# Two FFN stages of a fused kernel: rotations ahead of scalings at the end of a row, the MLP's norm earlier at its start

## The reference

```python
h = shift_token(x)                      # channels 64..127 from one token earlier
q, k, v = jnp.split(h @ wqkv, 3, axis=-1)   # 8 heads of 64
q = l2norm(q) * qs
k = l2norm(k) * ksc
q, k = rotary_xpos(q, k)
o = local_attention(q, k, v)            # windows of 64, each sees itself and the one before
x = x + o @ wo
h = shift_token(x)
h = (h - mu) / jnp.sqrt(var + 1e-05) * lg + lb
a, g = jnp.split(h @ w1 + b1, 2, axis=-1)
x = x + (a * jax.nn.gelu(g)) @ w2 + b2
```

## Time and profile before

| | |
|---|---|
| runs of the kernel | 2509.22, 2513.75, 2514.84 us (median 2513.75) |
| the profiled execution | 2516.16 us, span 2514.3 us, 43414 instructions |
| mean granted clock of TensorE | 0.885 |
| TensorE busy | 1950.6 us (78%) |
| VectorE busy | 1599.0 us (64%) |
| ScalarE busy | 1240.2 us (49%) |
| GpSimd busy | 1070.4 us (43%) |

### The profile page before, as it was taken

The page is one execution under the profiler, slowest core; times in us unless marked ns, Lnnn a source line. Parts: engine busy times, 40 slices in busy tenths (PEclk is TensorE's granted clock), DMA queues, the critical chain, the costliest instruction groups (busy, mean ns, idle before and its releaser), DMA issues.

```text
span 2514.3 us, 43414 instructions
## 1 busy us (share of the span) xinstructions
PE 1950.6 (78%) x14880; PEld 1224.8 (49%) x14880; DVE 1599.0 (64%) x2479; ACT 1240.2 (49%) x2826; POOL 1070.4 (43%) x838
## 2 busy tenths in 40 slices
PE   2788888858888986588888873896687888884596
PEld 1555555424555553355555532683344644642485
DVE  6677777556899796677777736584443344335486
ACT  2466655438999795465555543343322222224242
POOL 2555555335777675445655515132231033003333
PEclk9799999886999798789999985798898999896798
DMA  6000000020000001000000021204000000000202
GB/s 213 2 1 1 2 2 2 1 83 16 24 20 24 18 25 41 1 1 2 2 1 2 1 71 62 56 22 142 0 0 0 1 0 0 0 0 14 66 22 67
DMA packets 43928, 63.32 MB, mean 25 GB/s; under 512 B 7504, under 2 KB 33488, under 8 KB 42736
## 3 DMA queue, kind: packets, MB, share of 16 engines
q1 hardware_dynamic: 39232, 51.96, 6.6%
q0 software_dynamic: 4544, 9.35, 1.2%
HBM read 45.26 MB, written 21.18 MB: 26 GB/s over the span
## 4 chain that ended last, share of the span: by engine, by line
issue 30%; PE 19%; DVE 5%; ACT 3%; DMA 1%; SPq 1%; POOL 1%; DVEq 0%; POOLq 0%; ACTq 0%
PE PS L1721 3%; PE PS L448 2%; PE PS L1703 2%; PE PS L1705 1%; PE PS L1704 1%; DVE arena L756 1%; PE PS L1711 1%; PE PS L482 1%; DVE arena L769 1%; ACT arena L635 1%; PE PS L500 1%; PE PS L318 1%; PE PS L471 1%; DMA arena<-sorted_x 1%; PE PS L412 1%
## 5 line engine op out<-in xcount | busy, mean ns | idle before, releaser
L1495 POOL TENSOR_TENSOR arena<-arena 128x1024 f32<-128x1024 f32 x128 | 299.6, 2362 | 131.7 <-ACT arena L1429 131.7
L947 POOL TENSOR_TENSOR arena<-arena 128x512 f32<-128x512 f32 x128 | 132.8, 1040 | 263.7 <-DVE arena L790 261.8
L635 ACT ACTIVATE arena<-PS,arena 128x128 f32<-128x128 f32 x512 | 180.3, 370 | 125.3 <-DVE arena L783 124.9
L318 PE MATMUL PS<-arena_r 128*128 128x512 f32 x216 | 125.5, 581 | 135.2 <-DVE arena L756 63.8
L756 DVE SCALAR_TENSOR_TENSOR arena<-PS,fcol,big 128x512 f32<-128x512 f32 x256 | 177.3, 741 | 53.9 <-ACT arena L611 46.1
L1403 PE MATMUL PS<-con,arena 128*128 128x128 f32 x1024 | 157.2, 298 | 48.4 <-DVE arena L1479 46.0
L1479 DVE COPY arena<-PS 128x512 f32<-128x512 f32 x256 | 165.6, 684 | 21.3 <-PE PS L1403 21.2
L1403 PEld LDWEIGHTS PS<-con,arena 128*128 128x128 f32 x1024 | 118.8, 150 | 121.3 <-issue 94.6
L1429 ACT ACTIVATE arena<-PS,arena 128x512 f32<-128x512 f32 x256 | 154.9, 688 | 43.8 <-DVE arena L1460 42.1
L1440 ACT ACTIVATE arena<-arena 128x512 f32<-128x512 f32 x256 | 162.5, 636 | 23.3 <-DVE arena L1467 17.2
L2023 POOL DMA_INDIRECT expert_y<-arena x78 | 74.7, 958 | 209.3 <-DVE arena L1982 205.6
(11 more groups left out here) (366 smaller groups left out, 4924.3 us busy)
## 6 DMA issues: line engine op xcount, KB each, us to landing
big<-in_gu SPq DMA_DIRECT2D x16, 512.0 KB, 8.4
sorted_x<-in_slots SPq DMA_DIRECT2D x2, 2515.5 KB, 15.5
arena<-sorted_x SPq DMA_DIRECT2D x6, 774.0 KB, 7.6
big<-in_dn SPq DMA_DIRECT2D x16, 256.0 KB, 8.7
arena<-expert_y SPq DMA_DIRECT2D x16, 256.0 KB, 3.3
big<-in_wqkv SPq DMA_DIRECT2D x2, 1536.0 KB, 8.2
arena<-q_split SPq DMA_DIRECT2D x96, 32.0 KB
arena<-k_split SPq DMA_DIRECT2D x96, 32.0 KB
```

Of the source, the lines that this page charges most:

```text
L318: pe.matmul(bank, w_hi, hi, start=first, stop=False)
L635: act.activation(pr[:, u % 2, t, :], PS[:, u % 2, t * P:(t + 1) * P], ACT.Exp, bias=nmax[:, u % 2, t:t + 1], accum_out=psum_[:, u % 2, t:t ...
L947: g.tensor_tensor(pn[:, u % 2, :, :], pr[:, u % 2, :, :], pinv[:, u % 2, :].unsqueeze(2).broadcast_to([P, TPB, P]), ALU.mult).then_inc(s(" ...
L1495: g.tensor_tensor(a, a, mk[:, hp, 2 * half:2 * half + 2, :], ALU.mult).then_inc(s("a_masked"), 1)
```

## The change

On TensorE, the row's last values go ahead of the third norm's sum; at the start of the row, the MLP's mean goes ahead of the third value projection, and the variance ahead of the scores. On ScalarE, `hidden_input` moves to the end of the row before, the square ahead of the second unit's exponentials, and the last `take_heads` ahead of the third norm. On VectorE, the MLP's centring goes ahead of the copies of values, and `scaled(r, 3)` behind both; at the end of the row, the third and the fourth rotation go ahead of the first and the second scaling. POOL's list is the same, and nothing is added or removed.

```diff
@@ ffn_pe, row(r) @@
-                project_values(r, 0, 1, 2)
+                project_values(r, 0, 1)
                 if p is not None:
                     hidden_mean(p)
-                project_values(r, 3)
+                project_values(r, 2, 3)
                 turned(r, 0)
-                scores(r, 1)
                 if p is not None:
                     hidden_variance(p)
+                scores(r, 1)
                 turned(r, 1)
...
                 proj(3)
+                values(r, 3)
                 total(2)
-                values(r, 3)
                 if nx is not None:
                     scores(nx, 0)
                 attended(r)
@@ ffn_act, row(r) @@
                 if p is not None:
-                    hidden_input(p)
                     rnorm(r, 3)
                 take_values(r, 0)
+                if p is not None:
+                    ln_square(e_hidden(f, p))
                 exponentials(r, 1)
                 take_values(r, 2)
                 if p is not None:
-                    ln_square(e_hidden(f, p))
                     ln_rstd(e_hidden(f, p), 3)
...
                 norm(1)
                 square(2)
+                take_heads(r, 3)
                 norm(2)
-                take_heads(r, 3)
                 square(3)
                 if nx is not None:
                     exponentials(nx, 0)
+                    hidden_input(r)
@@ ffn_dve, row(r) @@
                 inverse(r, 0)
-                take_values(r, 1)
                 if p is not None:
                     hidden_centre(p)
+                take_values(r, 1)
+                take_values(r, 3)
+                if p is not None:
                     scaled(r, 3)
-                take_values(r, 3)
                 inverse(r, 1)
...
                 take_turned(r, 6)
-                scale(0)
                 rotated(2)
                 take_turned(r, 7)
+                scale(0)
+                rotated(3)
                 scale(1)
-                rotated(3)
                 if nx is not None:
                     maxima(nx, 0)
                     maxima(nx, 1)
                 scale(2)
                 attended(r)
```

## The result

| | before | after |
|---|---|---|
| median of the runs | 2511.56 us (4 runs) | 2616.96 us (4 runs, 2616.9 to 2621.04) |
| ratio, 95% interval | | 1.0423 [1.0399, 1.0447] |
| profiled execution, span | 2516.16, 2514.3 us | 2616.9, 2615.1 us |
| mean granted clock | 0.885 | 0.861 |

The kernel became slower by 4.2%, some 105 us. The forecast was slower, with 2571 us; the sign held and the size was a little over half of what came, outside the range.

A forecast was written before the change was run, and what follows sets the result against it. No engine is always busy; order and waits set the pace. Scores' delay +68, clock +28 and head -39 gave +57 us on the 2513.75 median: 2571 us, own range 2553 to 2590, overall range 2536 to 2600.

The forecast's parts named there:

- Step 1: Row's tail, VectorE: third rotation ahead of the first scaling lets the fourth projection start 0.57 us sooner.
- Steps 2 and 3: Row's tail: TensorE's third sum starts 0.51 us later, ScalarE's take_heads moves off the path; last squares come as before.
- Step 4: Row's tail, VectorE: scale(1), now behind the fourth rotation's second half, takes 2.0 us (1.7 to 2.8), ending at 234.9.
- Step 5: Row's tail, TensorE: next row's scores start 4.9 us late after 5.4 us idle; +68 us over 14 boundaries (+64 to +79).
- The head: Row's start: earlier mean, square and variance bring the gates 2.4 us sooner and end slow gates; -39 us (-24 to -48).
- step 3: Row's tail, ScalarE: later sum, earlier take_heads and norm cancel, so VectorE's second half of the fourth rotation starts at 231.5.
- The 2.1 us that the forecast sets beside its 2.0: Row's tail: scale(1)'s time if VectorE waits out POOL's sum under an exclusive port lock; 1 to 2 us in all.
- step 6: Scores after the long idle start at the low clock: +2.0 us each, +28 us; ends nothing and +45.
- B: Rival: low clock reaches through the output projection into the next head, gates stay slow; +89, 2603 us; chance 0.08.
- A: Rival: clock holds at the fourth projection after its 3.03 us wait, scores still late and slow; +29, 2543 us; chance 0.14.
- C: Rival: the clock never falls, despite both waits; at most +6 us, or -8 us, 2506 us; chance 0.08.
- D: Rival: scores(nx, 0) could start earlier if the scaling they wait for weren't the moved one; given nothing of its own.

The follow-up runs named there:

- scale1_first: The changed kernel with one pair of VectorE steps swapped back, scale(1) ahead of rotated(3); 2477.8 us, ratio 0.9866.
- head_alone: The kernel before with only the edits at the start of a row, the row's end as before; 2481.17 us, ratio 0.9864.
- fill_scores: The changed kernel with 16 unread mask matmuls on TensorE ahead of the next row's first scores; 2554.06 us, ratio 1.016.
- after_shift: The changed kernel with one extra VectorE reduction of 2048 columns at the end of the first FFN stage; 2598.78 us, ratio 1.034.
- before_fill: The kernel before with 14 unread mask matmuls in TensorE's 3.60 us wait ahead of the fourth projection; median 2489.51 us, ratio 0.9933.

## Why the prediction was right and wrong

**Right, step by step.** Step 1: the third rotation does come to stand in a wait for ScalarE (2.10 us), and the fourth projection gains 0.52 of the forecast 0.57 us. Steps 2 and 3: the last squares come no earlier. Step 4: `scale(1)` behind that half is what the scores wait for, 5.00 us for 5.4. Step 5 is confirmed by scale1_first, which undoes that one swap and removes the loss. The head: gates 2.0 us sooner in the row shown, and head_alone measures it at 32 us, inside the ends of 24 and 48.

In the row shown the delay of the scores, 4.9 us, came as forecast, in part by luck: VectorE's second half starts 243.75 - 236.41 = 7.34 us after the fourth projection, for 6.93 forecast, so the three moves of step 3 do not quite cancel, and `scale(1)` took 1.55 us for 2.0. That term was too high because of a row misread. The 1.70 us of the earlier trace rows had been taken as the price with POOL quiet, but POOL's copies ran beside it in the kernel before; with POOL idle it is 1.28 us.

```profile
185.43 0.61 POOL L962 COPY arena<-arena 64x512 f32<-64x512 f32 x1 [1.21 <-ACT arena L628]
186.20 0.88 POOL L966 COPY arena<-arena 64x512 f32<-64x512 f32 x1 [0.16 <-POOL arena L962]
```

The 2.1 us that the forecast sets beside its 2.0 have a slip as well: from 233.23 on, 1.70 us end at 234.93, which is 2.03 us behind 232.9.

**Wrong: step 6, the clock.** It took +2.0 us a row, for the scores alone, and kept the output projection at the full clock; its other end, 3.2 us a row, was "if the low level lasts on into the output projection". It lasts on in every boundary: +2.13 us for the scores and +2.04 for the output projection, 4.2 us a row and 58 us for 28, even above the end of 45. So the step that failed is the length of the low level in step 6: the sum put the output projection behind the scores at nothing. The upper end had been taken from the longest slow stretch in the earlier trace rows, 6.4 us. In the changed kernel the low level lasts 10.2 us in 13 of 14 boundaries; the scores fill 4.6 us of it, and it delays the output projection behind them by 1.3 to 2.8 us more. fill_scores shows that it is the clock, and that TensorE's idleness brings it.

**Smaller sizes.** Steps 4 and 5 were 0.5 us a row too high (-7 us): the delay is 4.6 to 4.9 us in nine boundaries but 3.6 to 3.7 in five. In those the kernel before already ran values and sum at the low level and took some 6.2 us to the scores, for 4.8 in the row shown, while the changed kernel took no longer than elsewhere. The forecast had worked out two rows and multiplied them by 14. The head was 0.55 too high (+8 us), most of it L301 beside POOL. With the clock's +30 this takes the +57 to +88, which is what the FFN stages give.

**Not foreseen: the attention stage.** 13 us of the result are from a stage that no step spoke of, and which takes 17 us less in after_shift with the same rows. No row of the FFN stages could have priced it; a range for a kernel whose attention stage has such stretches has to allow for one more or one less. It is not what missed the forecast: without it the +88 would give 2602 us, 31 above the forecast and still above 2600.

**The rivals.** B came nearest, with its mechanism (the clock reaches through the output projection) and 2603 us, but not in its second half: the head was quick, and the gates ran at full clock. That its +89 meets the +88 of the FFN stages is luck: its delay was 7 us too high, its clock 13 us too low and the gain of its head 7 us too small. A's condition was not met: in all 14 boundaries some 3 us or more of the 4.5 behind the fourth projection's start are at the low level, although its first matmul can still be at the full one (0.50 us in the row shown). What A had for it, slow gates after 2.49 us of idleness and full ones after 2.28, does not part the cases: in the kernel before one group ran slow after 2.21 us, and in before_fill gates after 2.49 us ran both ways. C and D fell. The one distance that was to part head from tail, from the output projection to the gates, did not: it is 15.0 us in the row shown, for 13.1 forecast and 15.5 before, because the slow output projection lies in it.

## What to carry to other kernels

Before a step is moved down an in-order engine, ask who waits for it, and what the steps now ahead of it wait for: here one scaling of 1.5 us, placed behind a wait that ran through three other engines, cost more than all else gained, and swapping it back gave a kernel faster than both. When a change opens a long idle time on TensorE, price the work behind it at the lower clock until a row shows it back at the full one, not just the first group of matmuls. And measure parts alone: a good half (the norm earlier, 32 us) was hidden under a bad one.

## What the runs showed of the hardware

- Matmuls whose result is thrown away made kernels faster by keeping the granted clock up through a wait: some 45 us in the FFN stages of the changed kernel (16 ahead of the scores), 0.7% in the kernel before (14 ahead of the fourth projection).
- In the attention stage the granted clock falls to the low level out of passes in which TensorE is busy 8.3 of 10 us; in the changed kernel and the kernel before it stays there for 30.7 us and costs some 12 us each time. Another piece begins ahead of the passes and lasts 37.5 us in the kernel before and 64.8 us in the changed one. With the same instructions the passes take 398 to 415 us over the 14 profiles. Differences of 10 to 20 us between two orders of this kernel say nothing of the orders until that stage has been compared.
- Two multiplications of 128x512 on VectorE took 1.28 us with POOL idle, 1.70 beside POOL's copies, and 2.37 and 2.83 beside its rotations.
